# Layer two's Hadamard transform: two of its three block rounds as signed products on TensorE, and the seed of the inverse root in one operation

## The reference, cut to what matters

```python
def fwht(x):                      # over the last dimension, n = 1024 here
    h = 1
    while h < n:
        x = x.reshape(-1, n // (2 * h), 2, h)
        a, b = (x[..., 0, :], x[..., 1, :])
        x = jnp.stack([a + b, a - b], axis=-2).reshape(-1, n)
        h *= 2
    return x / sqrt(n)
def bitlinear(x, w):   return einsum('bsh,oh->bso', act_quant(x), weight_quant(w))
def h_bitlinear(x, w): return einsum('bsh,oh->bso', act_quant(fwht(x)), weight_quant(w))
gate = bitlinear(x, w_gate)       # 256 -> 1024, weights -1, 0, 1 times a scale
up = bitlinear(x, w_up)
return h_bitlinear(silu(gate) * up, w_down)     # 1024 -> 256
```

## Time and profile before

| | us |
|---|---|
| median of 3 runs | 947.77 |
| lowest and highest of them | 940.79, 949.16 |
| the profiled execution | 944.57 |
| its span, first to last instruction | 942.7 |
| TensorE busy in it | 771.7 |
| VectorE busy | 562.8 |
| ScalarE busy | 340.4 |
| GpSimd busy | 174.5 |

### The profile page before, as it was taken

The page is one execution under the profiler, slowest core; times in us unless marked ns, Lnnn a source line. Parts: engine busy times, 40 slices in busy tenths (PEclk is TensorE's granted clock), DMA queues, the critical chain, the costliest instruction groups (busy, mean ns, idle before and its releaser), DMA issues.

```text
span 942.7 us, 13181 instructions
## 1 busy us (share of the span) xinstructions
PE 771.7 (82%) x4344; PEld 487.5 (52%) x4344; DVE 562.8 (60%) x1678; ACT 340.4 (36%) x576; POOL 174.5 (19%) x242
## 2 busy tenths in 40 slices
PE   2469979879778686469978887999888989998996
PEld 1244343467566365147655674556632323776774
DVE  3769898267568667546766126772176674732554
ACT  1333323564456463143310122122165868312220
POOL 0008514310010001000102203001204111051331
PEclk9756969989999788559999888999876999999998
DMA  8900000100000021000000020000000006012324
GB/s 236 315 2 1 1 0 1 44 2 3 1 2 2 1 90 46 0 1 1 1 1 1 1 92 0 1 2 1 0 2 2 2 3 180 7 68 79 107 74 156
DMA packets 33659, 36.05 MB, mean 38 GB/s; under 512 B 8456, under 2 KB 29913, under 8 KB 33593
## 3 DMA queue, kind: packets, MB, share of 16 engines
q1 hardware_dynamic: 31720, 30.08, 11.1%
q0 software_dynamic: 1872, 5.13, 1.5%
HBM read 25.78 MB, written 9.21 MB: 37 GB/s over the span
## 4 chain that ended last, share of the span: by engine, by line
PE 57%; DVE 24%; issue 7%; DVEq 5%; ACT 5%; DMA 1%; SPq 1%; POOL 0%; POOLq 0%; ACTq 0%
PE psum L1334 9%; PE psum L917 8%; PE psum L1389 4%; PE psum L1024 3%; PE psum L1360 3%; PE psum L1591 3%; PE psum L1364 3%; PE psum L1467 3%; PE psum L1433 3%; DVE arenas L2654 2%; PE psum L1605 2%; DVE arenas L2227 1%; DVE arenas L2357 1%; PE psum L1271 1%; PE psum L1306 1%
## 5 line engine op out<-in xcount | busy, mean ns | idle before, releaser
L1642 ACT ACTIVATE arenas<-psum 128x512 f32<-128x512 f32 (+5 forms) x86 | 59.5, 713 | 93.5 <-PE psum L917 68.8
L2654 DVE TENSOR_REDUCE arenas<-psum 128x2 f32<-128x512 f32 x96 | 61.9, 684 | 21.2 <-PE psum L1433 19.7
L1024 PE MATMUL psum<-early,arenas 128*128 128x512 f32 x128 | 67.8, 655 | 0.0
L917 PE MATMUL psum<-con,arenas 128*128 128x128 f32 (+1 forms) x204 | 33.6, 310 | 26.8 <-issue 13.5
L917 PE MATMUL psum<-conb,shared 128*128 128x128 bf16 (+2 forms) x512 | 38.0, 230 | 14.1 <-POOL shared L757 9.3
L755 POOL TENSOR_SCALAR arenas<-arenas,small 128x1024 f32<-128x1024 f32 x8 | 9.0, 1123 | 198.9 <-DVE small L2484 198.9
L1932 ACT ACTIVATE early<-psum 128x1024 f32<-128x1024 f32 x32 | 32.4, 1029 | 36.0 <-PE psum L1450 36.0
L1706 ACT ACTIVATE shared<-psum,small 128x256 f32<-128x256 f32 x64 | 26.8, 470 | 50.3 <-PE psum L1026 50.3
L917 PEld LDWEIGHTS psum<-conb,shared 128*128 128x128 bf16 (+2 forms) x512 | 33.1, 117 | 22.5 <-issue 11.1
L917 PEld LDWEIGHTS psum<-con,arenas 128*128 128x128 f32 (+1 forms) x204 | 25.9, 155 | 34.1 <-issue 31.1
L1334 PE MATMUL psum<-arenas,early 128*128 128x256 f32 (+1 forms) x192 | 43.3, 383 | 0.3 <-DVE arenas L2830 0.3
(11 more groups left out here) (373 smaller groups left out, 1811.5 us busy)
## 6 DMA issues: line engine op xcount, KB each, us to landing
early<-in_L_ffn_sw SPq DMA_DIRECT2D x3, 1024.0 KB, 12.4
late<-sorted_l SPq DMA_DIRECT2D x23, 129.0 KB, 2.1
sorted_l<-adj SPq DMA_DIRECT2D x1, 2944.0 KB, 20.8
early<-in_L_ffn_We_gate_up SPq DMA_DIRECT2D x2, 1408.0 KB
early<-in_L_ffn_expert_w SPq DMA_DIRECT2D x2, 1024.0 KB, 7.6
early<-in_L_ffn_w SPq DMA_DIRECT2D x1, 2048.0 KB, 8.4
late<-experts_l SPq DMA_DIRECT2D x4, 512.0 KB, 5.2
early<-in_L_ffn_Ws_gate_up SPq DMA_DIRECT2D x1, 1408.0 KB, 5.8
```

Source lines behind the costliest of these rows:

```text
L917: last = pe.transpose(v[0:parts, at:at + k], src, idn[0:k, 0:k])
L1024: pe.matmul(v, xnT[s][:, c * S + t * P:c * S + (t + 1) * P], ex_w[:, at:at + 2 * D], start=(c == 0), stop=False)
L1642: act.activation(dst, view(v), ACT.Copy, scale=scale).then_inc(f.drained(i, key), 1)
L2654: dve.tensor_reduce(nm, q3d(f.slot(0, ("max", w, k)), 2, S), X, ALU.max, negate=True)\
```

## The change

Two of the three rounds between blocks move from VectorE to TensorE. For each half of four blocks, TensorE accumulates in one bank the products of all four turned blocks, each with the matrix or its negative: output block m gets the sum over j of sign(j, m) times block j times the matrix. Block 0 goes to all four outputs in one product of 512 columns (the matrix as a repeated operand), blocks 1, 2 and 3 each in two products of 256 columns, whose moving operand is the matrix with its negative (`plus_minus`), the negative with the matrix (`minus_plus`), or one of them repeated. The negative and a second copy of the matrix are written by GpSimd over the two masks in `con`, once both parts of the setup are done. TensorE yields after each half instead of after both; its count of yields per tile stays four. VectorE keeps the first round (widths 512); its yields are moved so that the count stays four.

In `root_steps` the seed is made by one operation from the bits of the variance, and a `yield` and two operations with their drains go.

```diff
@@ -165,6 +165,8 @@
         ctx_all = sb("ctx_all", [P, B, T * C])
         con = sb("con", [P, 4 * P + E])
         ident, hadamard, iota8 = con[:, 0:P], con[:, P:2 * P], con[:, 4 * P:4 * P + E]
+
+        plus_minus, minus_plus, minus = con[:, P:3 * P], con[:, 2 * P:4 * P], con[:, 2 * P:3 * P]
         conb = sb("conb", [P, 4 * P], BF16)
         identb, mask_q, mask_k, onesb = (conb[:, k * P:(k + 1) * P] for k in range(4))
         bias3 = sb("bias3", [P, E * D], BF16)
@@ -226,7 +228,7 @@
             return v, [v[:, s * n:(s + 1) * n] for s in range(2)]
 
         st, mv = small.take(2 * T * 6).rearrange("p (n k) -> p n k", k=6), small.take(2 * T * 2).rearrange("p (n k) -> p n k", k=2)
-        var, seed, newton, rstd = (small.take(2 * T) for _ in range(4))
+        var, newton, rstd = (small.take(2 * T) for _ in range(3))
         (m8_all, m8), (idf_all, idf), (idx_all, idx) = cols(T, 8), cols(T, 2), cols(T, 8)
         idx_all, idx = idx_all.bitcast(U32), [v.bitcast(U32) for v in idx]
         (lg_all, lg), (oh_all, oh), (pick_all, pick), (cw_all, cw) = (cols(T, E) for _ in range(4))
@@ -682,6 +684,12 @@
             pool.memset(zeros, 0.0)
             pool.drain().then_inc(setup_ready, 1)
 
+
+            pool.wait_ge(setup_ready, 2)
+            pool.tensor_scalar(minus, hadamard, -1.0, None, ALU.mult)
+            pool.tensor_copy(con[:, 3 * P:4 * P], hadamard)
+            pool.drain()
+
             pool.wait_ge(wsum_ready, TURNS)
             pool.partition_all_reduce(wsums, wsum, P, bass.bass_isa.ReduceOp.add).then_inc(wsum_ready, 1)
 
@@ -1285,11 +1293,20 @@
                             pe.wait_ge(fc.drained(i, ("hT", s, t, h)), fc.read(i, ("hT", s, t, h)))
                             pe.wait_ge(fc.drained(i, ("had", s, t, h)), fc.empty(i, ("had", s, t, h)))
                             v = fc.slot(i, ("had", s, t, h))
-                            for j in range(4):
-                                at = t * H_FFN + (4 * h + j) * P
-                                mm = pe.matmul(v[:, j * P:(j + 1) * P], hb[s][:, at:at + P], hadamard, start=True, stop=True)
+
+                            for j, signs in enumerate(((hadamard,), (plus_minus, plus_minus), (hadamard, minus),
+                                                       (plus_minus, minus_plus))):
+                                at, n = t * H_FFN + (4 * h + j) * P, 4 // len(signs)
+                                for k, m in enumerate(signs):
+                                    m = m.rearrange("p (n k) -> p n k", k=P)
+                                    if m.shape[1] < n:
+                                        m = m.broadcast_to([P, n, P])
+                                    mm = pe.matmul(v[:, n * k * P:n * (k + 1) * P].rearrange("p (n k) -> p n k", k=P),
+                                                   hb[s][:, at:at + P], m, start=(j == 0), stop=(j == 3),
+                                                   skip_group_check=True)
                             mm.then_inc(fc.filled, 1)
-                        yield from steps(4)
+                            yield
+                        yield from steps(2)
                     if 0 <= step - 3 < 2 * T:
                         s, t = (step - 3) // T, (step - 3) % T
                         pe.wait_ge(yq_ready.sem, yq_ready.count(2 * i + s, t + 1))
@@ -2006,12 +2023,7 @@
 
                 dve.tensor_scalar(var, mv[:, :, 1], var_scale, eps, ALU.mult, ALU.add)
                 dve.drain()
-                dve.tensor_scalar(seed.bitcast(U32), var.bitcast(U32), 1, None, ALU.logical_shift_right)
-                dve.drain()
-                dve.tensor_copy(newton, seed.bitcast(U32))
-                dve.drain()
-                yield
-                dve.tensor_scalar(rstd.bitcast(U32), newton, -1.0, RSQRT_BITS, ALU.mult, ALU.add)
+                dve.tensor_scalar(rstd.bitcast(U32), var.bitcast(U32), -0.5, RSQRT_BITS, ALU.mult, ALU.add)
                 dve.drain()
 
                 dve.tensor_tensor(newton, rstd, rstd, ALU.mult)
@@ -2460,22 +2472,16 @@
 
                     dve.wait_ge(fc.drained(i, ("had", s, t, 0)), fc.read(i, ("had", s, t, 0)))
                     dve.wait_ge(fc.filled, fc.full(i, ("had", s, t, 1)))
-                    y, z, hi = ha[s][:, t * H_FFN:(t + 1) * H_FFN], bfly, fc.slot(i, ("had", s, t, 1))
+                    y, hi = ha[s][:, t * H_FFN:(t + 1) * H_FFN], fc.slot(i, ("had", s, t, 1))
                     dve.tensor_tensor(y[:, 4 * P:], y[:, 0:4 * P], hi, ALU.subtract)
                     dve.tensor_tensor(y[:, 0:4 * P], y[:, 0:4 * P], hi, ALU.add)\
                        .then_inc(fc.drained(i, ("had", s, t, 1)), 1)
                     dve.drain()
                     yield
-                    for src, dst, width in ((y, z, 2 * P), (z, y, P)):
-                        a = src.rearrange("p (n two w) -> p n two w", two=2, w=width)
-                        b = dst.rearrange("p (n two w) -> p n two w", two=2, w=width)
-                        dve.tensor_tensor(b[:, :, 0], a[:, :, 0], a[:, :, 1], ALU.add)
-                        dve.tensor_tensor(b[:, :, 1], a[:, :, 0], a[:, :, 1], ALU.subtract)
-                        dve.drain()
-                        yield
                     k = slice(t, t + 1)
                     dve.tensor_reduce(c1[s][:, k], y, X, ALU.max, apply_absolute_value=True)
                     dve.drain()
+                    yield
                     dve.tensor_scalar(c1[s][:, k], c1[s][:, k], H_FFN ** -0.5, EPS, ALU.mult, ALU.max)
                     dve.drain()
                     dve.reciprocal(c2[s][:, k], c1[s][:, k])
```

## The result

The changed kernel took 970.1 us in the median of four executions (968.74 to 971.52), the kernel before 947.42 beside it: the ratio is 1.0254, 95% interval 1.0214 to 1.0294. It is 2.5% slower, 24 us by the ratio; 966 was forecast, within 954 to 978. The profiled execution took 969.75 us, with a span of 967.9.

The account below looks back on a forecast made before the run. First pair: TensorE and VectorE wait for each other; second pair: TensorE is full. 7.4 + 18.8 - 5.4 = +20.8 us, from 944.57 profiled or 947.77 median to 965.4 or 968.6; forecast 966, own range 956 to 975, wider 954 to 978.

Parts of the forecast that it names:

- The added products: TensorE's Hadamard products in layer two's feed-forward: 3.44 us a half, 5.1 us added a tile, 40.8 us in all.
- First pair, +7.4: First pair of batches, 318.0 to 391.9 us: its own chain gets 7.4 us longer, 11.3 with no clock back.
- Second pair, +18.8: Second pair of batches, woven with layer three, TensorE full: 18.8 us longer, bounds 13.6 to 24.2.
- give-back: Second pair: TensorE's waits shrink by 2.1 us at 440.33 and about 1.4 us at 494.03.
- The new standing: Second pair: TensorE waits for a PSUM bank behind each tile's split products, +1.9 us over four tiles.
- The 1.4 us that I took back at 494.03: Second pair's 4.74 us wait at 494.03: VectorE's chain 2.74 + 0.49 shorter but starting 1.8 later, about 1.4 back.
- The seed, -5.4 beyond the pairs: Eleven roots on the last chain, outside the two pairs, each 0.49 us shorter: -5.4 us, or -3.
- GpSimd, 0: GpSimd's new wait, negation and copy at the start fall in its idle time and cost 0 us.
- The clock comes back: Rival: fuller TensorE keeps the clock full in later slow stretches, 9.4 us return, 956.0 us; chance 0.10.
- Nothing is given back: Rival: VectorE's shortened chain ends in waits, TensorE's waits move and the clock stays: +32.5, 977 us; chance 0.14.
- VectorE's chain is the bound: Rival: TensorE's waits take in the longer products, only gains of 28.3 us remain, 916 us; chance 0.03.
- The edit doesn't do what it says: Rival: for instance the repeated-block operand runs at half rate, 27.5 us more, 993 us; chance 0.03.

Follow-up runs that it names:

- the run in one piece: Changed kernel without the yield between the two halves' products, four yields behind them instead: 964.26 us, ratio 1.0204 to the kernel before.
- the mixing cut: VectorE's mixing put behind the down product's copy, except statistics and root: 932.32 us on the kernel before with new seed, 955.48 on the changed kernel without split.
- the signed kernel: The changed kernel, TensorE accumulating products with the matrix or its negative: 970.1 us, ratio 1.0254; run again 968.22 us, 1.0249.
- signed products alone: The changed kernel with the root's seed made by three operations as before, run twice: 978.14 us (1.0377) and 978.71 us (1.0365).
- the extra products: Kernel before plus six overwritten 256-column products per half on TensorE, VectorE's two rounds kept: 986.69 us, ratio 1.0447.

## Why the prediction was right, point by point

**The added products.** Right to the row: 3.45 us a half were measured, 3.44 priced; the 224 records and the full clock of the second pair as forecast. VectorE has 76 operations less, the 44 of the roots and the 32 of the two rounds.

**First pair, +7.4.** Measured +6.9 from its first product to its last down product. The chain held link by link. From the first products to tile two's are 14.2 us instead of 13.4, +0.9 by the unrounded starts, 1.1 worked out. Tiles two and three take from 350.84 to 373.74, 22.9 us, 23.1 worked out. From the down product to VectorE's start on tile four are 9.8 us, 9.9 worked out, and behind it the chain is 3.2 us shorter, as worked out. Both waits shrank (1.06 and 2.08 us, 0.7 and 2.0 worked out) and the work behind them is at full clock. That 15 us more of TensorE work cost only 7 is for the most part VectorE's rounds, which give 10.6 us in this pair when they alone are taken out.

**Second pair, +18.8.** Measured +21.1. This term was mis-sized by its give-back. The new standing is 0.30, 0.50, 0.49 and 0.31 us by the profile's modelled ends, 1.6 against 1.9, but the run in one piece says the split costs 3.2 us in this pair. The wait of 2.09 us became 0.69, not 0. The 1.4 us that I took back at 494.03 didn't come: the last wait grew by 0.82, and with the wait of 1.14 us ahead of the turn, which went, the standing there fell by 0.3. The mixing behind TensorE's own step sets it, and I had counted that chain from the end of the transform. The distance from that step to the last down product shows it: 10.20 us before and 10.22 without VectorE's rounds, 9.71 after and in one piece, 7.23 with the mixing cut. With these sizes the sum is 20.4 + 1.6 - 1.4 - 0.3 = 20.3 of the 21.1; 0.8 has no name.

**The seed, -5.4 beyond the pairs.** In the old kernel with the two of the pairs -5.0 measured, -6.4 by the sum; in the signed kernel -10.5. So that the whole came so near is in part luck, two errors of opposite sign: signed products alone cost +34 to +36 us (978.1 and 978.7 against 944.2 beside them; ratios 1.0377 and 1.0365), of which the pairs account for 7.4 + 22.0 = 29.4 (58.6 and 89.9 against 51.2 and 67.9) and my sum for 26.2 and the two roots of the pairs, 27.2; the seed gives back more than I took. The last 4 to 6 us of the signed products lie outside the pairs, where single profiles can't place them.

**GpSimd, 0.** Right: both operations end at 19 us, the reduction starts at 62.96.

**The rivals.** "The clock comes back" further on: it did not, 0.65 and 0.50 in the stretches that answer to the earlier trace rows:

```profile
399.30:410.50 11.20, 6.53 (x21) 1.91 (x22) 6.13 (x19) 3.94 (x6) 0.00 (x0) 0.65 0.00 0
416.20:427.10 10.90, 9.82 (x39) 7.91 (x41) 1.88 (x4) 7.82 (x11) 0.00 (x0) 0.50 0.00 0
```

The waits of 3.31 and 4.26 us that shrank to 1.06 and 2.08 were followed by full clock afterwards. The rule of the Trainium skill (page "TensorE: Matmul & The Clock Gate", section "HAM oscillation — how this bites in real kernels"), that waits between bursts of matmuls drop the clock, agrees with that. With the extra products, though, the work right behind the same wait of 3.31 us is at full clock (0.60 us for two products, 1.03 before), so the wait's length alone doesn't decide it. "Nothing is given back": the two-by-two of products and rounds excludes it. Removing the rounds gives 9.4 us with short products; with long ones it gives 11 to 17 (986.7 less 964.3, less 5 to 11 for the seed), in the cut spans 13.1 in the first pair and 2.2 in the second, of which the seed alone had 0.5 and 0.7. "VectorE's chain is the bound": taking its two rounds out saves 0.8 us in the second pair with short products and about 1.5 with long ones, and the extra products are paid nearly in full in both pairs, so no. "The edit doesn't do what it says": a half takes 3.45 us, so the operand with repeated blocks runs at the same rate as one without.

## What to carry to other kernels

Price an edit per stretch, by who is late there: 15.3 us more of TensorE work cost 7 us where VectorE's rounds, moved out of the same chain, gave back 10.6; with nothing moved out, 18.8 and 20.1 of 20.6 us were paid. Work that leaves an engine pays only where that engine is late by its own work; where its next wait is for the other engine, here the mixing behind layer three's step, the time goes into that wait. And what stands in the queue ahead of a small operation for which another engine waits can be worth as much as moving arithmetic away: cutting the mixing behind its root gave 6 to 9 us, 5.0 of them in the pairs, and VectorE's two rounds are worth 9.4 at no cost to TensorE.

## What the runs showed of the hardware that had not been expected

A wait of 1.7 us ahead of the down product was followed by full clock in the second pair (1.92 us) and by half clock in the first (3.60 us). What stood before differs: in the second pair TensorE had been busy for 60.0 of 62.9 us at full clock, in the first it had waited 7.06 us, and then worked for one, shortly before:

```profile
377.96 1.03 PE L917 MATMUL psum<-conb,shared 128*128 128x128 bf16 x8 [7.06 <-POOL shared L757]
```

Nor does one and the same wait tell the clock behind it. Ahead of the same turn of the first pair TensorE waits 4.33 us in the signed kernel in one piece and in that with the mixing cut; the eight turns behind it take 0.65 us in the one and 1.04 in the other:

```profile
386.30 0.65 PE L925 MATMUL psum<-conb,shared 128*128 128x128 bf16 x8 [4.33 <-POOL shared L765]
```

```profile
387.80 1.04 PE L925 MATMUL psum<-conb,shared 128*128 128x128 bf16 x8 [4.33 <-POOL shared L765]
```

What decides it, no run here shows.

The same kernel's profiled execution differed by 3.2 us ahead of layer two and 3.6 us behind it, and by 0.1 us in the 147 us of the two pairs.
